# An attention kernel whose row maxima run four blocks ahead of the exponents' own head instead of five

## What is computed

```
xn = layernorm(x)
q, k, v = split(xn @ w_qkv.T)              # 16 heads of 16 columns, 2 batches
attn = softmax(rope(q) @ rope(k).T / 4)    # 2 x 16 heads, each 2048 x 2048
s = (attn @ v) @ w_out.T
g = silu(experts(xn))                      # each token goes to one of 8 experts
out = x + s * g
```

## Time and profile before

| | |
|---|---|
| median of 3 runs | 1448.64 us (1447.99 to 1452.01) |
| profiled execution | 1446.31 us, its span 1444.5 us |
| PE, DVE, ACT busy | 1421.2, 1335.9, 1189.2 us |
| TensorE clock granted | full speed in all slices that the profile shows |

### The profile page before, as it was taken

How to read it: one execution, slowest core, us unless ns; L and a number is a source line. 1 busy time by engine, 2 the same in 40 slices (tenths; PEclk the granted TensorE clock), 3 DMA queues, 4 the chain that set the end, 5 groups by cost and what they waited for, 6 DMA issues and landing times.

```text
span 1444.5 us, 31854 instructions
## 1 busy us (share of the span) xinstructions
PE 1421.2 (98%) x11152; PEld 632.7 (44%) x11152; DVE 1335.9 (92%) x1910; ACT 1189.2 (82%) x2382; POOL 179.9 (12%) x288
## 2 busy tenths in 40 slices
PE   8999999999999999999999999999999999999988
PEld 5555444443474344444444444444444444444326
DVE  7789999999948999999999999999999999999807
ACT  5553588888878999898899889989888888998990
POOL 5433322200011111111110000000100000000110
PEclk9999999999999999999999999999999999999999
DMA  6774244427263354333333353332333522333323
GB/s 232 257 206 131 67 89 82 78 46 133 48 206 75 64 119 68 64 64 64 64 49 49 51 106 49 45 46 42 43 47 47 108 46 46 44 45 42 71 71 120
DMA packets 80344, 120.06 MB, mean 83 GB/s; under 512 B 28994, under 2 KB 66754, under 8 KB 73282
## 3 DMA queue, kind: packets, MB, share of 16 engines
q1 hardware_dynamic: 74258, 106.34, 37.0%
q0 software_dynamic: 3072, 8.39, 2.4%
q10 hardware_dynamic: 2896, 3.62, 0.7%
HBM read 77.67 MB, written 39.71 MB: 81 GB/s over the span
## 4 chain that ended last, share of the span: by engine, by line
PE 81%; DVE 14%; ACT 2%; issue 1%; DMA 1%; SPq 0%; POOL 0%; POOLq 0%; ACTq 0%
PE ps L1302 34%; PE ps L1316 31%; DVE arena L832 6%; DVE arena L835 6%; PE ps L1290 4%; PE ps L1218 3%; ACT arena L679 2%; PE ps L1516 2%; PE ps L1219 1%; PE ps L1450 1%; PE ps L1251 1%; PE ps L1243 1%; PE ps L1479 1%; PE ps L1405 1%; PE ps L1230 1%
## 5 line engine op out<-in xcount | busy, mean ns | idle before, releaser
L1290 PE MATMUL ps<-ks,qs 48*128 48x512 f32 x1984 | 684.3, 442 | 0.6 <-DVE arena L835 0.4
L1302 PE MATMUL ps<-qs,ks 50*128 50x512 f32 x2048 | 679.7, 435 | 0.5 <-ACT arena L660 0.5
L832 DVE TENSOR_REDUCE arena<-ps 128x1 f32<-128x512 f32 x992 | 655.5, 720 | 5.3 <-PE ps L1290 5.1
L835 DVE TENSOR_REDUCE arena<-ps 128x1 f32<-128x1024 f32 x496 | 623.0, 1256 | 0.9 <-PE ps L1290 0.9
L679 ACT ACTIVATE arena<-ps 128x512 f32<-128x512 f32 x1056 | 564.4, 605 | 60.1 <-PE ps L1302 49.9
L679 ACT ACTIVATE x_sb<-ps 128x512 f32<-128x512 f32 x992 | 535.3, 598 | 59.0 <-PE ps L1302 42.2
L1302 PEld LDWEIGHTS ps<-qs,ks 50*128 50x128 f32 x2048 | 329.2, 184 | 476.5 <-issue 163.4
L1290 PEld LDWEIGHTS ps<-ks,qs 48*128 48x128 f32 x1984 | 326.2, 184 | 8.8 <-DVE arena L832 3.5
L1316 PE MATMUL ps<-arena 128*32 128x256 f32 (+1 forms) x3104 | 307.6, 468 | 5.4 <-ACT arena L679 4.1
L1316 PE MATMUL ps<-x_sb,arena 128*32 128x256 f32 (+1 forms) x2960 | 290.2, 464 | 0.0
L1316 PEld LDWEIGHTS ps<-arena 128*32 128x32 f32 x3104 | 62.3, 107 | 124.5 <-issue 124.5
(11 more groups left out here) (123 smaller groups left out, 626.3 us busy)
## 6 DMA issues: line engine op xcount, KB each, us to landing
qs<-parts_d SPq DMA_DIRECT2D x186, 128.0 KB
ks<-parts_d SPq DMA_DIRECT2D x186, 128.0 KB
parts_d<-arena SPq DMA_DIRECT2D x64, 256.0 KB, 3.0
xs_d<-arena SPq DMA_DIRECT2D x13, 384.0 KB, 3.7
arena<-xs_d SPq DMA_DIRECT2D x13, 384.0 KB, 3.5
ys_d<-arena SPq DMA_DIRECT2D x13, 384.0 KB, 2.8
x_sb<-in_x SPq DMA_DIRECT2D x2, 2048.0 KB, 13.1
onum_d<-arena SPq DMA_DIRECT2D x124, 32.0 KB
```

Of the source, the lines that this page charges most:

```text
L832: nc.vector.tensor_reduce(most[head_slot][:, tile, u:u + 1], ps[:, AB + lo, :], AX.X, ALU.max).then_inc(a_reduced[u], 1)
L835: nc.vector.tensor_reduce(most[head_slot][:, tile, u:u + 1], ps[:, AB + lo:AB + hi, :], AX.XY, ALU.max).then_inc(a_reduced[u], 1)
L1290: ins = nc.tensor.matmul(ps[:, AB + c, :], qs[head_slot][ABASE:ABASE + KR, tile * P:(tile + 1) * P].bitcast(F32R), ks[head_slot][ABASE:ABA ...
L1302: nc.tensor.matmul(ps[:, bank, :], ks[s][at:at + KS, kb * P:(kb + 1) * P].bitcast(F32R), qs[s][at:at + KS, c * W:(c + 1) * W].bitcast(F32R ...
```

## The change

One constant goes from five blocks to four:

```diff
     PVB = 3
     AB = 4
-    AHEAD = KB + 5
+    AHEAD = KB + 4
     GROUPS = ((0, 1), (1, 2), (2, 4))
```

## The result

After takes 1485.6 us in the median of 4 runs (1484.19 to 1489.49), before 1449.26 (1447.99 to 1452.01). The ratio is 1.0255, with an interval of 1.0239 to 1.027: 36 us slower. The forecast had the sign and the mechanism, and 1472.2 as the number; the range ended at 1481.

The account below looks back on a forecast made before the run. DVE, without a gap in the long loop, was taken as the bound. Waits 22.5, slow issues 0.6, opening 0.8 and end -0.35 summed to +23.6 us, on a median of 1448.64 giving 1472.2; range 1461 to 1481.

Parts of the forecast that it names:

- The margin and the wait: Maxima's DMAs to next head's B0: a 1.44 us margin, landing 2.33 later, becomes a PE wait of 0.89 us.
- What reaches DVE: In each long-loop head A1, not A0, comes too late for its reduction: 0.79 us of gap on DVE.
- the 0.1 of cover taken off for A1: A1's end to its reduction: about 0.1 us of slack, subtracted from the 0.89 wait to give 0.79.
- heads 1 to 5: The DVE gap there, with a margin of 1.54 us: 0.69 us a head, 3.5 us together.
- one slow issue: Four DMA issues taking 0.3 us longer, now without margin; expected twice in 29 heads, 0.6 us.
- The opening: Counts stand ahead of the last opening maxima block, PE waits for POOL, and DVE is 0.8 us late.
- The end: Last head: DMA way unchanged, ACT begins 0.35 us sooner with nothing left over from the block before: -0.35 us.
- the clock falls in the waits: Rival: PE's pause in each head halves its clock, 31 us on top, 1503 us or more; chance 0.03.
- heads 7 to 30: The DVE gap in these 24 long-loop heads: 0.79 us each, 19.0 us together.

Follow-up runs that it names:

- Two, four and six small DMAs: Kernel before, with two, four or six 4 KB writes to scratch on SP's queue ahead of each head's four DMAs (not head 0's): 1451.73, 1460.79, 1511.67 us.
- the run of the opening alone: Kernel before, five blocks ahead, with counts and first three B one maxima block earlier and that block's fillers gone: 1454.55 us, ratio 1.0028.
- the run with fillers: After, with three repeated A0 matmuls on PE ahead of each wait for the maxima's DMAs, nine ahead of the last head's: 1476.19 us, ratio 1.0191.
- three blocks: After with the same constant one less again, three blocks ahead: 1656.95 us, ratio 1.1419 against before.
- two of the DMAs on ACT: After, four blocks ahead, with two of each head's four DMAs issued by ACT in place of SP: 1499.79 us, ratio 1.0332.
- six blocks: Kernel before with the lead raised from five blocks to six: 1456.34 us, ratio 1.0031.

## Why the prediction was wrong, point by point

- **The margin and the wait were right.** 1.44 us of margin, 2.33 later, a wait of 0.89: measured are 0.76 us of idle PE and 1.85 from issue to B0 in the head shown. Two, four and six small DMAs find the margin's edge where 1.44 puts it: by the heads' lengths 0.83 are free, 1.75 cost 0.30 a head, 2.68 cost 1.24.
- **What reaches DVE was right.** 0.77 us a head for 0.79; A1 and not A0 runs dry. The modelled ends could be trusted to 0.1 us here, but not further: the 0.1 of cover taken off for A1 isn't seen with the small DMAs, which cost all that goes beyond the margin. With the clock up, heads 1 to 5 lose 4.3 us where 3.5 and one slow issue (0.3) were forecast.
- **The opening** costs what was worked out on DVE: from the first reduction of the block ahead of the counts to that of the last block it is 160.80 - 157.07 = 3.73 us in the rows below, and was 3.03, 0.7 for 0.8. In the run of the opening alone some 3 us by the clock come to it, which were not in the sum.

```profile
157.07 1.28 DVE L832 TENSOR_REDUCE arena<-ps 128x1 f32<-128x512 f32 x2
...
160.80 1.29 DVE L832 TENSOR_REDUCE arena<-ps 128x1 f32<-128x512 f32 x2 [1.25 <-PE ps L1290]
```

- **The end** was right but for the clock. The -0.35 us counted ACT's head start; PE's pause ahead of the last B0, 2.24 us, was not priced. It came with a clock of 0.57 for 12 us behind it, and the stretch behind DVE's last reduction became 2.9 us longer. In the run with fillers it is 0.25 shorter than before, close to the forecast.
- **The step that failed is the rival "the clock falls in the waits"**, put at 0.03 and kept out of the sum. What it put at nothing is some 11 us of the median (the sum below). I had one row against it, a pause of 1.04 us in a stretch at a clock of 1.00. One pause without a fall isn't evidence that 29 pauses have none. In after's profiled execution a fall stands behind the waits of 2 heads of 29, one of 1.33 us and one of 0.80, among pauses of 0.75 to 1.33. With six small DMAs it is 6 of 29 (pauses of 1.0 to 1.4, and 3.3 in head 1), with three blocks all of them (3.1 to 3.8). A longer pause brings more falls, but its length doesn't decide alone: with two of the DMAs on ACT ten falls stand behind pauses of 0.83 to 1.8. The rival's price was wrong as well: it had 1.07 us for a fall in each of 29 heads, and the two falls cost 4.3 and 1.5 (the second is in head 2, which lasts 40.72 us, and 39.17 with the fillers).

The sum then: after's median clock is 0.9875, 2 x 0.0125 x 1485 = 37 us at half speed, 14.5 us at 0.39 each; before's is 0.997 (taken from its later runs), 3.4 us. So 11 of the 36.3 us are the clock's, and 25 remain for 23.6 of the forecast.

The profiled executions show the same by place. The table has by how much after falls further behind in each stretch, read from the end of the same maxima block's reduction (L835) in both traces, and for the last stretch from the spans:

| us | forecast | after | with fillers at the waits |
|---|---|---|---|
| ahead of the opening, where the kernels are alike | 0 | 2.0 | -0.4 |
| opening | 0.8 | 2.0 | 2.4 |
| heads 1 to 5 | 3.5 | 5.9 | 4.3 |
| around the expert stage | 0 | 1.4 | 0.0 |
| heads 7 to 30, slow issues included | 19.6 | 24.5 | 20.3 |
| behind the last reduction | -0.35 | 2.9 | -0.25 |
| sum | 23.6 | 38.7 | 26.4 |

Between after and the run with fillers lies 12.3 us. In each stretch where after is the later by more than a microsecond its trace has a stretch at half speed that the other has not. Two of these don't stand behind a wait that the change made. The one ahead of the opening (2.0) is also in the profiles with two and with four small DMAs, whose kernels are those of before up to there. The one around the expert stage (1.4) is in four of the six profiles at four blocks and in none at five; what makes it is open. The change's own falls in the loop and at the end make some 9 us in this execution: 1.5, 4.3 and 3.2.

The falls behind the waits in the loop and at the end are shown to come from what PE leaves undone (fillers take them away, and 8 to 10 us of the median with them). What makes the clock fall in the opening is open. It did in the profile of every kernel whose opening differs from that of before, with three, four and six blocks and with the opening alone, and in no profile whose opening is the same. But two fillers ahead of the pause didn't prevent it, and with six blocks PE has no pause over 0.4 us there.

No version beats the kernel before. In its long loop DVE has no gap, and a longer lead only leaves more B behind the last maxima.

## What to carry to other kernels

What a step of lead is worth is the lateness that it takes off the longest way between two streams, and nothing beyond the margin: with 1.44 us of margin 0.83 us cost nothing here, and 2.33 cost 0.77 a head. Work out the margin from the start of the last issue to the first waiter, and compare it with the step. Where a wait is put on an engine that feeds the bound one, look for the consumer behind the longest product on that engine's queue; here it was the one without cover. And price PE's pauses a second time, by the clock: a chance of a fall for each pause times its cost (in after 1.5 to 4.3 us), with many pauses in a run, even if one pause in the trace had none.

## What the runs showed of the hardware that was not expected

- The granted clock falls behind pauses of PE of under a microsecond too, but only behind some: 29 pauses of 0.75 to 1.33 us gave two falls in the profiled execution, behind one of 0.80 and one of 1.33. At the low level a score took 0.79 for 0.50 and the product with the values 1.93 for 1.06. The Trainium skill's page "TensorE: Matmul & The Clock Gate", Part 1, has two levels, and the rows agree with it: within a fall the granted clock is 0.50 (602 to 611 us of after), outside 1.00, and no record of these traces has a third.
- Three repeated matmuls in a pause of 0.8 us kept the clock at 1.00 over 915 us.
- A 4 KB DMA from a constant tile to DRAM holds SP's queue for 0.42 to 0.45 us (six take 2.68), one into two rows of a stack in 128-byte pieces for 0.66 (four take 2.62).
